# A graph network kernel on one core: the message sum as products of split operands, moved behind two state products

## The chip, the cores and the metric

The kernel runs on one core of a Trainium2 chip. The metric is the device time of one execution in microseconds, the median over runs. TensorE (PE) multiplies into PSUM, VectorE (DVE), ScalarE (ACT) and GpSimd (POOL) do the elementwise work, SyncE (SP) issues the loads and stores. Each engine works through its own instruction list in order; the lists meet at semaphores.

## The reference, cut to what matters

Sixteen graphs of 512 nodes with 128 features, each with a 512x512 weighted adjacency.

```python
x = x + L0_gnn(layernorm(x), adj)          # relu(norm_adj @ (x W + b))
x = x + layernorm(x) @ Wf.T + bf
x = x + L1_gnn(layernorm(x), adj)          # below
x = x + L1_ffn(layernorm(x))               # 30 steps of tanh, silu, layernorm, 128x128 product

# L1_gnn, per graph:
x_conv = relu(conv17(relu(conv1(x))) + x)          # with folded batch norms
A   = exp(-dist(s, s)) * mask                       # s = x w_se.T; mask is adj: the edges
msg = relu(x @ w_msg.T + b_msg)
x_nmp = A @ msg                                     # the edge-weighted message sum
gi, gh = [x_conv, x_nmp] @ w_ih.T + b_ih, x @ w_hh.T + b_hh
r, z = sigmoid(gi_r + gh_r), sigmoid(gi_z + gh_z)
out = (1 - z) * tanh(gi_n + r * gh_n) + z * x
```

## The kernel before, in words

Two stages: the graph stage (to about 545 us), one step per graph, and the 30 feed-forward iterations, which work on all nodes in eight groups. The change touches the graph stage only.

A step `step(b, p, c, d)` does, software pipelined, the L1 graph layer of graph b, the L0 graph layer and linear layer of graph c = b + 1, and the adjacency of graph d = b + 2. There is no planner: the order of every engine is written out by hand in its own `step` function (POOL L544, PE L713, ACT L1035, DVE L1426). A wait therefore holds everything behind it on its engine. Steps 0 and 1 and the last ones are written apart; the middle ones run in a loop.

Numbers: a plain fp32 product is one call with fp32 operands. Where the kernel wants the other way it keeps an operand as two parts of type fp32r, the high part (a copy rounded to fp32r, by ScalarE) and the low part (the operand less the high part, by VectorE or POOL), and `product` (L676) issues three matmuls: high x high, high x low, low x high. conv1, the convolution, the state products (HH, three gates on x) and the input products (IH, on x_conv and x_nmp) are of that kind. The message sum (L844 to 851) is not: four fp32 products of 128x512, one for each edge tile mt, out of `msg_tok` and `edge`.

Order on TensorE in the last third of a step: distances 0 and 1, adjacency turns 0 and 1 (transposes into the banks TURN_A and TURN_B), turn(1) of the layernorm, distances 2 and 3, the linear layer's products, the last convolution tap, the message sum, turns 2 and 3, nine matmuls of the state products (DIST_A, DIST_B, TURN_B), six of x_conv, turn(2), then the x_nmp products and the next step's conv1.

What feeds them. ScalarE: exp(0..3) into `edge`, adjacency copies 0 and 2 out of TURN_A (`adjt_even`), the two relus of x_conv, x_nmp's high part, gates. VectorE: edge products 1 and 3 (L1306, edge times adjacency), adjacency copies 1 and 3 out of TURN_B (`adjt_odd`, L1302), statistics (L1264) and norms (L1295), conv_sum (L1422), x_nmp's low part (L1568). POOL: edge products 0 and 2 (L509), the small `rstd` pairs (L503, L505) between statistics and norms, x_conv's low part (L596). The third turn waits for the first copy, as both use TURN_A. Each adjacency copy overwrites the tile from which the step's edge products are made: `adj_t[p]` is shared by graphs b and d, and a copy of any tile waits for all of the step's edge products (L990 to 994, L1299 to 1302).

Of the kernel before, what the change touches and what calls it, by code (L numbers as in the profile page):

```python
# [27 lines left out]
P = 128  # L28
# [63 lines left out]
def build(nc, x, adj, w0, b0, wf, bf, w_se, b_se, conv1_w, bn1, conv2_w, bn2, w_msg, b_msg,  # L92
          w_ih, b_ih, w_hh, b_hh, ln_w, ln_b, w1, b1, out):
    with ExitStack() as ctx:
# [26 lines left out]

            return sba(name + "_h", shape, F32R), sba(name + "_l", shape, F32R)

        work = sba("work", [P, 20 * N])

        def piece(first, count):
            return work[:, first * N:(first + count) * N]
# [52 lines left out]

        emb_m = sba("emb_m", [KD, N], F32R)
        emb_n = sba("emb_n", [KD, N], F32R)
        emb_f = [[sba(f"emb_f{w}{k}", [KD, N]) for k in range(2)] for w in range(2)]
        msg_tok = sba("msg_tok", [P, NT, C])
        conv_pre = sba("conv_pre", [P, N])
        x_conv = split("x_conv", [P, N])
        x_nmp = split("x_nmp", [P, N])
        n_act = sba("n_act", [P, N])
        upd = sba("upd", [P, N])


# [83 lines left out]
        s_exp = sem("s_exp")  # L275
        s_edge_p = sem("s_edge_p")
        s_edge_v = sem("s_edge_v")
        s_nmp = sem("s_nmp")
        s_x_nmp = sem("s_x_nmp")
        s_x_nmp_lo = sem("s_x_nmp_lo")  # L280
# [189 lines left out]
        def _(pool):  # L470
# [36 lines left out]
            def edges(b, p, mt):  # L507
                pool.wait_ge(s_exp, 4 * b + mt + 1)
                pool.tensor_tensor(edge[:, mt, :], edge[:, mt, :], adj_t[p][:, mt, :], ALU.mult).then_inc(s_edge_p, 1)  # L509

            def power(j):
                pool.wait_ge(f_v, j + 1)
                half = slice(GT * (j % 2), GT * (j % 2) + GT)
                pool.tensor_tensor(f_rs[:, both(j), half], f_var[:, j, :], half_neg[:, 0:GT], ALU.pow).then_inc(f_pow, 1)
# [29 lines left out]
            def step(b, p, c, d):  # L544
                l1 = exists(b)
                if l1:

                    pool.wait_ge(s_h1, 2 * b + 1)
                    if c is not None:
                        pool.wait_ge(s_xs, c + 1)  # L550
                    inner = slice(EDGE, EDGE + INNER)
                    odd = phases(h_full[:])[:, 1, inner]
                    for k in range(2):
                        even = phases(h_full[:, 2 * k:2 * k + 2 * (EDGE + INNER)])[:, 0, inner]
                        ins = pool.tensor_tensor(diff[:, k, inner], even, odd, ALU.subtract)
                    ins.then_inc(s_diff, 1)
                    pool.wait_ge(s_diff_hi, b + 1)
                    pool.tensor_tensor(diff_s[1][:, :, inner], diff[:, :, inner], diff_s[0][:, :, inner].bitcast(F32),
                                       ALU.subtract).then_inc(s_diff_lo, 1)
                    for w in range(2):  # L560
                        pool.wait_ge(s_emb_sg, 2 * b + w + 1)
                        pool.tensor_tensor(emb_f[w][0][:], emb_f[w][0][:], emb_f[w][1][:], ALU.mult).then_inc(s_emb_v, 1)

                if b is None and c is not None:
                    pool.wait_ge(s_wload, 16 * NWEIGHTS)

                    pool.wait_ge(s_xs, 1)
                    for k in range(SUM_FILLS):
                        even, odd = (conv2_nat[:, :, 8 * k + h:8 * k + h + 7:2].rearrange("p i t -> p t i") for h in range(2))
                        pool.tensor_tensor(sum_nat[k], even, odd, ALU.add).then_inc(s_sums, 1)  # L570
                if c is not None:
                    rstd(1, c)
                if b is None:
                    rstd(0, d)
                if b is None and c is not None:
                    vectors()
                if l1:
                    if c is not None:

                        pool.wait_ge(s_norm[1], c + 1)  # L580
                    edges(b, p, 0)
                if later(b) and not ends(b, B - 1):
                    rstd(3, b - 1)
                if ends(b, B):
                    power(2)
                    power(3)
                    centre(2, 2)
                if l1:
                    edges(b, p, 2)
                if c is not None:  # L590
                    rstd(2, c)
# [27 lines left out]
        def _(pe):  # L619
# [93 lines left out]
            def step(b, p, c, d):  # L713
# [126 lines left out]
                        pe.wait_ge(s_rows_read, 1)  # L840
                    turn_adjacency(0, 2)
                if l1:

                    pe.wait_ge(s_msg_tok, b + 1)  # L844
                    for mt in range(NT):
                        if mt % 2 == 0:
                            pe.wait_ge(s_edge_p, 2 * b + mt // 2 + 1)
                        else:
                            pe.wait_ge(s_edge_v, 2 * b + mt // 2 + 1)
                        m = pe.matmul(bank[CHAN], msg_tok[:, mt, :], edge[:, mt, :], start=(mt == 0), stop=(mt == NT - 1))  # L850
                    m.then_inc(s_nmp, 1)
                if d is not None:
                    turn_adjacency(2, NT)
                if l1:
                    x_in = cut(xc_s, 0, N)

                    pe.wait_ge(s_exp, 4 * b + 4)
                    product(bank[DIST_A], w(HH), x_in, stop=False)
                    product(bank[DIST_B], w(HH + 1), x_in, stop=False)
                    if d is not None:  # L860
                        pe.wait_ge(s_adjt_odd, 2 * d + 2)
                    elif not l0:
                        pe.wait_ge(s_gh_n, b)
# [95 lines left out]
        def _(act):  # L959
# [29 lines left out]

            def adjt_even(c, q, mt):  # L990
                act.wait_ge(s_adj_turned, 4 * c + mt + 1)
                wait(act, s_edge_p, 2 * (c - 1))
                wait(act, s_edge_v, 2 * (c - 1))
                act.activation(adj_t[q][:, mt, :], bank[TURN_A], ACT.Copy).then_inc(s_adjt_even, 1)

            def exp(b, mt):
                act.wait_ge(s_dist, 4 * b + mt + 1)
                wait(act, s_nmp, b)
                act.activation(edge[:, mt, :], bank[DIST_A + mt % 2], ACT.Exp).then_inc(s_exp, 1)  # L999

            def silu(j, s):
                act.wait_ge(f_u, s + 1)
# [32 lines left out]
            def step(b, p, c, d):  # L1035
# [37 lines left out]
                if l1:  # L1073
# [4 lines left out]
                        act.activation(emb[:], emb_f[m][0][:], ACT.Copy).then_inc(s_emb_hi, 1)  # L1078
                    act.wait_ge(s_msg_pre, b + 1)
                    wait(act, s_nmp, b)  # L1080
                    act.activation(msg_tok[:], msg_tok[:], ACT.Relu).then_inc(s_msg_tok, 1)
                    if ends(b, B - 1):
                        silu(0, 0)
                        silu(1, 1)
# [11 lines left out]
                if l1:  # L1096
                    exp(b, 2)
                    exp(b, 3)
                if d is not None:
                    adjt_even(d, p, 0)  # L1100
                if l1:
                    act.wait_ge(s_conv_pre, b + 1)
                    wait(act, s_z_ps, b)
                    act.activation(x_conv[0][:], conv_pre[:], ACT.Relu, bias=vec(SH2)).then_inc(s_x_conv, 1)
# [1 line left out]
                    act.activation(conv_pre[:], conv_pre[:], ACT.Relu, bias=vec(SH2)).then_inc(s_x_conv, 1)  # L1106
                if ends(b, B - 1):
                    tanh(0, 2)
                if l1:
                    act.wait_ge(s_nmp, b + 1)  # L1110
                    act.activation(x_nmp[0][:], bank[CHAN], ACT.Copy).then_inc(s_x_nmp, 1)
                if ends(b, B - 1):
                    tanh(0, 3)
                if d is not None:
                    adjt_even(d, p, 2)
                if l1:

                    act.wait_ge(s_ghn_ps, b + 1)
# [30 lines left out]
        def _(dve):  # L1149
# [148 lines left out]

            def adjt_odd(c, q, mt):  # L1299
                dve.wait_ge(s_adj_turned, 4 * c + mt + 1)  # L1300
                wait(dve, s_edge_p, 2 * (c - 1))
                dve.tensor_copy(adj_t[q][:, mt, :], bank[TURN_B]).then_inc(s_adjt_odd, 1)  # L1302

            def edges(b, p, mt):
                dve.wait_ge(s_exp, 4 * b + mt + 1)
                dve.tensor_tensor(edge[:, mt, :], edge[:, mt, :], adj_t[p][:, mt, :], ALU.mult).then_inc(s_edge_v, 1)  # L1306

            def statistics_of(j, s, q):
                if q == 0:
# [116 lines left out]
            def step(b, p, c, d):  # L1426
# [96 lines left out]
                    conv_sum(b)  # L1523
                if l1:
                    edges(b, p, 1)
                if later(b) and not ends(b, B - 1):
                    dve.wait_ge(s_x3, b)
                    stats(3, b - 1)
# [2 lines left out]
                if l0:  # L1531
# [1 line left out]
                    dve.tensor_tensor(x_graph(c), x_graph(c), tiles(bank[TOK]), ALU.add).then_inc(s_x2, 1)  # L1533
                    dve.wait_ge(s_x2, c + 1)
                    stats(2, c)
                if d is not None:
                    adjt_odd(d, p, 1)
                if l1 and not ends(b, B - 1):
                    conv_sum(b)
                if ends(b, B - 1):  # L1540
                    statistics(1, 1)
                    scaled_sum(0, 2)
# [77 lines left out]
```

## Time and profile before

| | us |
|---|---|
| median of 3 runs | 1264.63 (1263.76 to 1265.21) |
| the profiled execution's own time | 1265.02 |
| its span, first to last instruction | 1263.0 |
| busy: PE, DVE, ACT, POOL | 1228.0, 1151.7, 960.0, 947.3 |
| mean granted TensorE clock | 0.993 of full |

How to read the rows: a timeline row has start and duration in us, the engine, the line of the kernel, the operation, the tile written and the tiles read, and how many such instructions are merged (x4 means the duration runs over four). Square brackets tell how long the engine was idle before it and which instruction, on which line, ended the wait. A matmul's duration contains its drain, so the cost of one in a stream is the distance between starts. The tile `work` holds the adjacency, its copies and `edge` in one buffer; names alone do not tell them apart, lines do.

### The profile page before, as it was taken

To read this page: it belongs to the slowest core of one execution; us is meant where nothing else is said; L and a number is where in the kernel's file an instruction comes from. 1 tells how busy PE (TensorE), PEld (TensorE's weight loads), DVE (VectorE), ACT (ScalarE), POOL (GpSimd) and SP (SyncE) were. 2 spreads that over 40 slices of the span, in tenths; PEclk is the share of its full clock that TensorE was granted. 3 is DMA by queue.
4 is the path that set the end of the run, shared out by engine and by line. 5 is a ranking of instruction groups with operands and counts; after the bars stand their busy time and mean duration, and the time that the engine had idled before them with its cause. 6 is when DMAs were issued, how large, how long until landed. Compare 5 with 4: busy or idle time off the path is not lost.

```text
span 1263.0 us, 27914 instructions
## 1 busy us (share of the span) xinstructions
PE 1228.0 (97%) x9073; PEld 1094.9 (87%) x9073; DVE 1151.7 (91%) x3029; ACT 960.0 (76%) x1170; POOL 947.3 (75%) x667
## 2 busy tenths in 40 slices
PE   8899999999999999869999999999999999999998
PEld 7677777777777777659999999999999999999998
DVE  7988888888888887789999999999999999999996
ACT  2455555555555555769999999999999999999994
POOL 2455555555555555579999999999999999999996
PEclk9999999999999999979999999999999999999999
DMA  6111111111111000000000000000000000000004
GB/s 196 43 43 42 43 42 42 42 42 42 43 42 46 35 0 1 1 1 1 1 0 0 0 0 0 0 0 0 0 0 0 0 0 0 0 0 0 0 0 133
DMA packets 29812, 27.77 MB, mean 22 GB/s; under 512 B 3285, under 2 KB 21464, under 8 KB 29656
## 3 DMA queue, kind: packets, MB, share of 16 engines
q1 hardware_dynamic: 29784, 27.41, 6.9%
q8 instruction: 16, 0.26, 0.1%
q14 instruction: 12, 0.10, 0.0%
HBM read 23.21 MB, written 4.19 MB: 22 GB/s over the span
## 4 chain that ended last, share of the span: by engine, by line
PE 74%; DVE 13%; issue 5%; ACT 4%; POOL 3%; DVEq 0%; DMA 0%; SPq 0%; POOLq 0%; ACTq 0%
PE psum L894 28%; PE psum L946 15%; PE psum L679 4%; PE psum L681 4%; PE psum L680 4%; PE psum L850 4%; PE psum L911 3%; PE psum L701 3%; PE psum L696 3%; POOL h_ring L533 2%; DVE emb_n L1507 2%; DVE xh_mem L1295 1%; PE psum L690 1%; ACT emb_f L1054 1%; DVE u_ring L1329 1%
## 5 line engine op out<-in xcount | busy, mean ns | idle before, releaser
L533 POOL TENSOR_TENSOR h_ring<-g_pair,f_rs 128x1024 f32<-128x1024 f32 x240 | 451.9, 1904 | 31.5 <-DVE f_rs L1400 19.0
L1312 DVE BATCH_NORM_STATS2 f_stat<-g_pair 128x6 f32<-128x256 f32 x960 | 394.5, 425 | 2.4 <-ACT g_pair L1003 2.4
L946 PE MATMUL psum<-ident,h_ring 128*128 128x128 f32 (+1 forms) x1920 | 296.8, 277 | 7.8 <-POOL h_ring L533 6.8
L1329 DVE SCALAR_TENSOR_TENSOR u_ring<-t_ring,psum 128x1024 f32<-128x1024 f32 x232 | 281.9, 1215 | 8.1 <-ACT t_ring L1013 3.6
L946 PEld LDWEIGHTS psum<-ident,h_ring 128*128 128x128 f32 (+1 forms) x1920 | 247.7, 167 | 35.1 <-issue 7.1
L1017 ACT ACTIVATE y_all<-psum 128x1024 f32<-128x1024 f32 x240 | 244.0, 1017 | 17.2 <-PE psum L946 17.2
L894 PE MATMUL psum<-w_t,y_all 128*128 128x128 f32 x1920 | 254.5, 276 | 0.0
L894 PE MATMUL psum<-w1c_t,y_all 128*128 128x128 f32 x1920 | 253.8, 275 | 0.0
L1003 ACT ACTIVATE g_pair<-u_ring 128x1024 f32<-128x1024 f32 x240 | 251.7, 1049 | 0.9 <-DVE u_ring L1329 0.9
L1013 ACT ACTIVATE t_ring<-psum 128x1024 f32<-128x1024 f32 x232 | 238.1, 1026 | 15.6 <-PE psum L894 8.9
L894 PEld LDWEIGHTS psum<-w_t,y_all 128*128 128x128 f32 x1920 | 234.3, 192 | 0.0
L894 PEld LDWEIGHTS psum<-w1c_t,y_all 128*128 128x128 f32 x1920 | 233.7, 192 | 0.0
L523 POOL TENSOR_TENSOR g_pair<-g_pair,f_stat 128x1024 f32<-128x1024 f32 x120 | 229.8, 1915 | 0.0
L503 POOL TENSOR_SCALAR ln_ve<-ln_stat 128x4 f32<-128x4 f32 x64 | 19.4, 303 | 135.9 <-DVE ln_stat L1264 135.9
L999 ACT ACTIVATE work<-psum 128x512 f32<-128x512 f32 x64 | 34.8, 595 | 96.1 <-PE psum L761 96.0
L911 PE MATMUL psum<-bias,ones_bf 65*128 65x512 bf16 x240 | 91.9, 383 | 0.0
L679 PE MATMUL psum<-diff_s_h,wt_h 128*128 128x256 f32 x272 | 81.2, 299 | 0.0
L680 PE MATMUL psum<-diff_s_l,wt_h 128*128 128x256 f32 x272 | 76.4, 281 | 0.0
L681 PE MATMUL psum<-diff_s_h,wt_l 128*128 128x256 f32 x272 | 76.3, 280 | 0.0
L505 POOL TENSOR_TENSOR ln_rs<-ln_ve,half_neg 128x4 f32<-128x4 f32 x64 | 71.7, 1120 | 5.3
L509 POOL TENSOR_TENSOR work<-work 128x512 f32<-128x512 f32 x32 | 46.5, 1456 | 32.7 <-DVE xh_mem L1295 25.4
L1366 DVE TENSOR_REDUCE f_share<-psum 128x16 f32<-128x48 f32 x354 | 67.5, 191 | 0.1
(200 smaller groups left out, 2146.7 us busy)
## 6 DMA issues: line engine op xcount, KB each, us to landing
work<-in_adj_dram SPq DMA_DIRECT2D x16, 1024.0 KB, 5.5
x_tok<-in_x_dram SPq DMA_DIRECT2D x16, 256.0 KB, 5.6
out_dram<-y_all SPq DMA_DIRECT2D x7, 512.0 KB, 3.2
work<-in_L_gnn_conv_w_dram SPq DMA_DIRECT2D x1, 1088.0 KB
out_dram<-y_all SPq DMA_DIRECT2D x2, 256.0 KB, 3.6
work<-in_L_gnn_w_ih_dram SPq DMA_DIRECT2D x1, 384.0 KB
work<-in_L_gnn_w_hh_dram SPq DMA_DIRECT2D x1, 192.0 KB
work<-in_L_gnn_W_dram SPq DMA_DIRECT2D x1, 64.0 KB, 5.1
```

The source lines that it names most:

```text
L523: pool.tensor_tensor(two, two, means, ALU.subtract).then_inc(f_mean, 1)
L533: pool.tensor_tensor(tiles(h_ring[j % 4]), tiles(g_ring[j]), spread(f_rs[:, both(j), at:at + GT], GT, C), ALU.mult).then_inc(f_norm, 1)
L679: pe.matmul(dst, lhs[0], rhs[0], start=start, stop=False)
L680: pe.matmul(dst, lhs[0], rhs[1], start=False, stop=False)
L894: m = pe.matmul(y_ps[k % 2][:, h, C * t:C * t + C], y_all[:, GT * k + NT * h + t, :], w1c_t[:] if h == centred(k) else w1_t[:], start=(h = ...
L911: pe.matmul(y_ps[k % 2][:, 1 - centred(k), :].rearrange("p (o n) -> p o n", o=2), ones_bf[:], four, start=True, stop=False, skip_group_che ...
L946: m = pe.transpose(g_ps[j % 2][0:rows, t // NT, P * (t % NT):P * (t % NT) + P], tiles(h_ring[j % 4])[:, t, 0:rows], ident[:])
L1003: act.activation(g_ring[j], u_ring[j % 2], ACT.Silu).then_inc(f_silu, 1)
L1013: act.activation(t_ring[k % 2], src, ACT.Tanh).then_inc(f_tanh, 1)
L1017: act.activation(y_all[:, GT * j:GT * j + GT, :].rearrange("p t c -> p (t c)"), g_ps[j % 2].rearrange("p h n -> p (h n)"), ACT.Copy).then_ ...
L1312: ins = dve.bn_stats(f_stat[:, j, 0, 2 * q:2 * q + 2, :].rearrange("p t w -> p (t w)"), two)
L1329: dve.scalar_tensor_tensor(out=u_ring[k % 2], in0=t_ring[k % 2], scalar=STEP, in1=src, op0=ALU.mult, op1=ALU.add).then_inc(f_u, 1)
```

## The change

The messages and the edges are split into high and low parts, and each edge tile's sum is a `product` of three matmuls, in the order 1, 0, 3, 2. The state products of r and z and turns 2 and 3 go ahead of the message sum. ScalarE makes the high parts, with a new wait for the update of graph b-1 (whose `n_act` shares memory with `msg_h`); the low parts of edges 0 and 2 and of the messages go to POOL, those of edges 1 and 3 to VectorE. An adjacency copy waits only for the edge product of its own tile; copy 1 on VectorE and copy 2 on ScalarE come earlier in their lists. Buffers: `edge_l` lies over `edge`, `edge_h` over `emb_f`, `msg_l` over `msg_tok`, `msg_h` over `n_act`.

```diff
 # POOL
+            def edge_low(b, mt):
+                pool.wait_ge(s_edge_hi_p, 2 * b + mt // 2 + 1)
+                pool.tensor_tensor(edge_l[:, mt, :], edge[:, mt, :], edge_h[:, mt, :].bitcast(F32),
+                                   ALU.subtract).then_inc(s_edge_lo_p, 1)
+            def msg_low(b):
+                pool.wait_ge(s_msg_hi, 2 * b + 2)
+                pool.tensor_tensor(msg_l[:], msg_tok[:], msg_h[:].bitcast(F32),
+                                   ALU.subtract).then_inc(s_msg_tok, 1)
...
+                if l1:
+                    msg_low(b)
                 if c is not None:
                     rstd(1, c)
...
                 if l1:
                     edges(b, p, 2)
+                    edge_low(b, 0)
+                    edge_low(b, 2)
                 if c is not None:
                     rstd(2, c)
 # PE
                 if l1:
-                    pe.wait_ge(s_msg_tok, b + 1)
-                    for mt in range(NT):
-                        if mt % 2 == 0:
-                            pe.wait_ge(s_edge_p, 2 * b + mt // 2 + 1)
-                        else:
-                            pe.wait_ge(s_edge_v, 2 * b + mt // 2 + 1)
-                        m = pe.matmul(bank[CHAN], msg_tok[:, mt, :], edge[:, mt, :], start=(mt == 0), stop=(mt == NT - 1))
-                    m.then_inc(s_nmp, 1)
-                if d is not None:
-                    turn_adjacency(2, NT)
-                if l1:
                     x_in = cut(xc_s, 0, N)
                     pe.wait_ge(s_exp, 4 * b + 4)
                     product(bank[DIST_A], w(HH), x_in, stop=False)
                     product(bank[DIST_B], w(HH + 1), x_in, stop=False)
+                if d is not None:
+                    turn_adjacency(2, NT)
+                if l1:
+                    pe.wait_ge(s_msg_tok, b + 1)
+                    for mt in (1, 0, 3, 2):
+                        if mt % 2 == 0:
+                            pe.wait_ge(s_edge_lo_p, 2 * b + mt // 2 + 1)
+                        else:
+                            pe.wait_ge(s_edge_lo_v, 2 * b + mt // 2 + 1)
+                        m = product(bank[CHAN], (msg_h[:, mt, :], msg_l[:, mt, :]), (edge_h[:, mt, :], edge_l[:, mt, :]),
+                                    start=(mt == 1), stop=(mt == 2))
+                    m.then_inc(s_nmp, 1)
 # ACT
             def adjt_even(c, q, mt):
                 act.wait_ge(s_adj_turned, 4 * c + mt + 1)
-                wait(act, s_edge_p, 2 * (c - 1))
-                wait(act, s_edge_v, 2 * (c - 1))
+                if isinstance(c, int) and c < 2:
+                    pass
+                else:
+                    act.wait_ge(s_edge_p, 2 * (c - 2) + mt // 2 + 1)
...
+                    if later(b):
+                        act.wait_ge(s_upd, b)
+                    act.activation(msg_h[:], msg_tok[:], ACT.Relu).then_inc(s_msg_hi, 1)
+                    act.wait_ge(s_msg_hi, 2 * b + 1)
+                    act.activation(msg_tok[:], msg_tok[:], ACT.Relu).then_inc(s_msg_hi, 1)
...
                     exp(b, 3)
+                    edge_high(b, 0)
                 if d is not None:
                     adjt_even(d, p, 0)
                 if l1:
+                    edge_high(b, 1)
+                    edge_high(b, 3)
+                    edge_high(b, 2)
                     act.wait_ge(s_conv_pre, b + 1)
 # DVE
             def adjt_odd(c, q, mt):
-                wait(dve, s_edge_p, 2 * (c - 1))
+                if not (isinstance(c, int) and c < 2):
+                    dve.wait_ge(s_edge_v, 2 * (c - 2) + mt // 2 + 1)
...
                 if l1:
                     edges(b, p, 1)
+                if d is not None and l1:
+                    adjt_odd(d, p, 1)
...
-                if d is not None:
+                if d is not None and not l1:
                     adjt_odd(d, p, 1)
+                if l1:
+                    edge_low(b, 1)
                 if l1 and not ends(b, B - 1):
                     conv_sum(b)
+                if l1:
+                    edge_low(b, 3)
```

`edge_high` on ScalarE is a Copy of one edge tile to fp32r behind that tile's edge product; VectorE's `edge_low` is POOL's with its own semaphores. On ScalarE `adjt_even(d, p, 2)` moves from behind x_nmp's high part to before it.

## Rows read from the trace of the kernel before

**Rows 1.** Busy time by stretch: stretch, length, PE, PEld, DVE, ACT, POOL, clock.
```profile
60.00:480.00 420.00, 416.91 (x2442) 330.27 (x2441) 351.80 (x672) 217.06 (x363) 216.08 (x244) 1.00 0.12 38
```

**Rows 2.** Timeline of TensorE, step 8 and the start of step 9.
```profile
289.85 0.40 PE L679 MATMUL psum<-xc_s_h,wt_h 128*128 128x512 f32 x1
...
309.93 3.60 PE L850 MATMUL psum<-work,msg_tok 128*128 128x512 f32 x8
313.36 1.04 PE L710 MATMUL psum<-ident,work 128*128 128x128 f32 x8
...
316.33 0.40 PE L679 MATMUL psum<-x_conv_h,wt_h 128*128 128x512 f32 x1
...
317.74 0.60 PE L690 MATMUL psum<-ident,xh_mem 128*128 128x128 f32 x4
318.24 0.47 PE L679 MATMUL psum<-x_nmp_h,wt_h 128*128 128x512 f32 x1
...
321.13 0.39 PE L679 MATMUL psum<-xc_s_h,wt_h 128*128 128x512 f32 x1
```

**Rows 3.** Timeline of POOL, step 8.
```profile
304.11 1.43 POOL L505 TENSOR_TENSOR ln_rs<-ln_ve,half_neg 128x4 f32<-128x4 f32 x1
307.28 1.64 POOL L509 TENSOR_TENSOR work<-work 128x512 f32<-128x512 f32 x1 [1.74 <-DVE xh_mem L1295]
...
310.14 1.30 POOL L509 TENSOR_TENSOR work<-work 128x512 f32<-128x512 f32 x1
...
312.31 1.07 POOL L505 TENSOR_TENSOR ln_rs<-ln_ve,half_neg 128x4 f32<-128x4 f32 x1
314.68 1.29 POOL L596 TENSOR_TENSOR x_conv_l<-conv_pre,x_conv_h 128x512 fp32r<-128x512 f32 x1 [1.30 <-ACT conv_pre L1106]
```

**Rows 4.** Timeline of VectorE, step 8, and two rows of step 9.
```profile
307.08 0.69 DVE L1306 TENSOR_TENSOR work<-work 128x512 f32<-128x512 f32 x1
...
309.63 0.69 DVE L1306 TENSOR_TENSOR work<-work 128x512 f32<-128x512 f32 x1 [1.17 <-ACT work L999]
...
311.07 0.76 DVE L1264 BATCH_NORM_STATS2 ln_stat<-x_tok 128x6 f32 x2 [0.15 <-DVE x_tok L1533]
311.75 0.68 DVE L1302 COPY work<-psum 128x512 f32<-128x512 f32 x1
312.34 0.75 DVE L1422 SCALAR_TENSOR_TENSOR conv_pre<-psum,bcol,conv_pre 128x512 f32<-128x512 f32 x1
...
315.04 1.78 DVE L1295 TENSOR_SCALAR xh_mem<-x_tok,ln_stat,ln_rs 128x128 f32 x4
...
317.42 0.67 DVE L1568 TENSOR_TENSOR x_nmp_l<-psum,x_nmp_h 128x512 fp32r<-128x512 f32 x1
...
330.79 0.69 DVE L1479 SCALAR_TENSOR_TENSOR upd<-upd,n_act 128x512 f32<-128x512 f32 x1
...
332.77 0.69 DVE L1496 SCALAR_TENSOR_TENSOR x_tok<-agg_tok,x_tok 128x512 f32 x1
```

**Rows 5.** Timeline of ScalarE, step 8.
```profile
297.81 0.64 ACT L1078 ACTIVATE emb_m<-emb_f 105x512 fp32r<-105x512 f32 x1
...
305.96 1.09 ACT L999 ACTIVATE work<-psum 128x512 f32<-128x512 f32 x2 [6.47 <-PE psum L761]
...
311.48 0.60 ACT L994 ACTIVATE work<-psum 128x512 f32<-128x512 f32 x1 [1.88 <-POOL work L509]
```

**Rows 6.** Timeline of VectorE, step 0 and step 15.
```profile
59.59 1.38 DVE L1306 TENSOR_TENSOR work<-work 128x512 f32<-128x512 f32 x1 [0.62 <-ACT work L999]
...
514.65 0.69 DVE L1476 SCALAR_TENSOR_TENSOR upd<-gates,upd 128x512 f32<-128x512 f32 x1
515.38 1.66 DVE L1479 SCALAR_TENSOR_TENSOR upd<-upd,n_act 128x512 f32<-128x512 f32 x1
```

**Rows 7.** Timeline of POOL, step 0 and step 15.
```profile
59.15 1.27 POOL L509 TENSOR_TENSOR work<-work 128x512 f32<-128x512 f32 x1 [0.73 <-ACT work L999]
...
514.72 1.76 POOL L562 TENSOR_TENSOR emb_f<-emb_f 105x512 f32<-105x512 f32 x1 [0.65 <-ACT emb_f L1054]
```

More of the change, by code:

```diff
@@ L122, in split @@
             return sba(name + "_h", shape, F32R), sba(name + "_l", shape, F32R)
-        work = sba("work", [P, 20 * N])
+        with ExitStack() as under:
+            work = under.enter_context(nc.sbuf_tensor("work", [P, 20 * N], F32))
+        sba("work_below", [P, 16 * N])
+        edge_l = sba("edge_l", [P, NT, N], F32R)
         def piece(first, count):
@@ L182, in build @@
         emb_n = sba("emb_n", [KD, N], F32R)
-        emb_f = [[sba(f"emb_f{w}{k}", [KD, N]) for k in range(2)] for w in range(2)]
-        msg_tok = sba("msg_tok", [P, NT, C])
+        with ExitStack() as under:
+            emb_f = [[under.enter_context(nc.sbuf_tensor(f"emb_f{w}{k}", [KD, N], F32)) for k in range(2)] for w in range(2)]
+            msg_tok = under.enter_context(nc.sbuf_tensor("msg_tok", [P, NT, C], F32))
+        edge_h = sba("edge_h", [P, NT, N], F32R)
+        msg_l = sba("msg_l", [P, NT, C], F32R)
         conv_pre = sba("conv_pre", [P, N])
@@ L187, in build @@
         x_nmp = split("x_nmp", [P, N])
-        n_act = sba("n_act", [P, N])
+        with ExitStack() as under:
+            n_act = under.enter_context(nc.sbuf_tensor("n_act", [P, N], F32))
+        msg_h = sba("msg_h", [P, NT, C], F32R)
         upd = sba("upd", [P, N])
@@ L277, in build @@
         s_edge_v = sem("s_edge_v")
+        s_edge_hi_p = sem("s_edge_hi_p")
+        s_edge_hi_v = sem("s_edge_hi_v")
+        s_edge_lo_p = sem("s_edge_lo_p")
+        s_edge_lo_v = sem("s_edge_lo_v")
+        s_msg_hi = sem("s_msg_hi")
         s_nmp = sem("s_nmp")
@@ L999, in exp, with edge_high @@
                 act.activation(edge[:, mt, :], bank[DIST_A + mt % 2], ACT.Exp).then_inc(s_exp, 1)
+            def edge_high(b, mt):
+                if mt % 2 == 0:
+                    act.wait_ge(s_edge_p, 2 * b + mt // 2 + 1)
+                else:
+                    act.wait_ge(s_edge_v, 2 * b + mt // 2 + 1)
+                act.activation(edge_h[:, mt, :], edge[:, mt, :], ACT.Copy).then_inc(s_edge_hi_p if mt % 2 == 0 else s_edge_hi_v, 1)
             def silu(j, s):
@@ L1080, in step @@
                     wait(act, s_nmp, b)
-                    act.activation(msg_tok[:], msg_tok[:], ACT.Relu).then_inc(s_msg_tok, 1)
+                    if later(b):
[3 more added lines that the diff above has]
+                    act.activation(msg_tok[:], msg_tok[:], ACT.Relu).then_inc(s_msg_hi, 1)
                     if ends(b, B - 1):
@@ L1108, in step @@
                     tanh(0, 2)
+                if d is not None:
+                    adjt_even(d, p, 2)
                 if l1:
@@ L1113, in step @@
                     tanh(0, 3)
-                if d is not None:
-                    adjt_even(d, p, 2)
                 if l1:
@@ L1306, in edges, with edge_low @@
                 dve.tensor_tensor(edge[:, mt, :], edge[:, mt, :], adj_t[p][:, mt, :], ALU.mult).then_inc(s_edge_v, 1)
+            def edge_low(b, mt):
+                dve.wait_ge(s_edge_hi_v, 2 * b + mt // 2 + 1)
+                dve.tensor_tensor(edge_l[:, mt, :], edge[:, mt, :], edge_h[:, mt, :].bitcast(F32),
+                                  ALU.subtract).then_inc(s_edge_lo_v, 1)
             def statistics_of(j, s, q):
@@ L1535, in step @@
                     stats(2, c)
-                if d is not None:
+                if d is not None and not l1:
                     adjt_odd(d, p, 1)
+                if l1:
+                    edge_low(b, 1)
                 if l1 and not ends(b, B - 1):
                     conv_sum(b)
+                if l1:
+                    edge_low(b, 3)
                 if ends(b, B - 1):
```

## The prediction

> **What bounds the kernel now.** I read the busy time by stretches first. From 60 to 480 us, the graph stage in its steady state, TensorE is busy 416.91 of 420.00 us at full granted clock; VectorE is at 352, ScalarE at 217, POOL (GpSimd) at 216 [rows 1]. So there TensorE's order of work is the time, and another engine costs only what it makes TensorE wait. I followed one of the sixteen steps, b = 8, in the timeline of each engine. TensorE starts its conv1 product at 289.85 and the next step's at 321.13: a period of 31.28 us [rows 2]. In it: message products 309.93 to 313.36 (3.43 us for four fp32 products, eight records), two adjacency turns and nine state products to 316.33, six x_conv products to 317.74 (1.41, so 0.235 each), a turn, and the x_nmp products from 318.24. All times below are of this step.
>
> Two cross-engine inputs arrive only just in time there. x_conv_l ends on POOL at 314.68 + 1.29 = 315.97 [rows 3], 0.36 before TensorE takes it. x_nmp_l ends on VectorE at 317.42 + 0.67 = 318.09 [rows 4], 0.15 before TensorE takes it. These two margins are what the change must not eat.
>
> **TensorE's part.** Four fp32 products (3.43 us) go; twelve fp32r products of 128x512 come, 12 x 0.235 = 2.82. The state products and turns only change places. Gain 0.61 us a step, 16 x 0.61 = 9.8 us in all, if nothing waits. By that order the state products of r and z run 309.93 to 311.34, the turns (2.97 for turns and nine products, less 9 x 0.235: 0.85) to 312.2, messages to 315.0, the third state product to 315.7, and TensorE would want x_conv_l at 315.7 and x_nmp_l at 317.6.
>
> **What comes on the other engines, per step.**
> - ScalarE: four edge roundings and one more message rounding, at the 0.64 of a copy of that kind [rows 5]: 3.2 us. It is half idle, and the message pair runs in the 6.47 us in which it waits for the distances: its new wait for upd (331.48 in step 9, so 300.2 here [rows 4]) holds only the first exp behind it, at 305.96. The edge roundings stand behind the last exp (309.6) with the first adjacency copy between them, five operations at about 0.6: three are done by 311.8, the last waits for POOL's second edge product. Nothing queued behind them is late: x_conv waits for conv_sum anyway. Cost 0 by itself.
> - The adjacency copies wait only for their own tile. ScalarE's 1.88 us wait before the first copy [rows 5] goes; it was idle time of an engine with room, so 0. But the copy is now behind one rounding (done about 310.8), which TensorE needs before the third turn at 311.34: covered by 0.5. The adjacency loads on SP's queue, released by the turns, go out some 2 us earlier, as the turns now come before the messages; their first reader is in the next step. 0.
> - VectorE: two edge_low of 0.69 (the kind of its edge product, two SBUF inputs); a copy of 0.68 moves forward, ahead of the statistics for graph b-1 [rows 4].
> - POOL: msg_low and two edge_low, each a 128x512 difference, at the 1.30 of x_conv_l and of the second edge product [rows 3]: 3.9 us. The two edge_low stand in POOL's queue behind its second edge product and ahead of rstd(2) and of x_conv_l. That is the step of the change which I hold to decide.
>
> **POOL's queue alone, a floor.** From the first edge product's start at 307.28 nothing before is changed. Then 1.64 (blocked as now), rstd(3) 1.3 (its second operation is 1.07, the first and the gap 0.2), edge product 1.30, two edge_low 2.60, rstd(2) 1.3, x_conv_l 1.29: 9.4 us without any wait, so x_conv_l is not done before 316.7, where TensorE had begun on it at 316.33. The rest up to the next step is fixed TensorE work: +0.4 us a step at least, though TensorE has 0.61 less to do. With rstd(3) half a us later, since its statistics stand behind the moved copy, it is 317.25 and +1.0.
>
> **The two engines block one another.** At 59.15 POOL's edge product runs to 60.42; VectorE's, started at 59.59, takes 1.38 instead of 0.69 and ends at 60.97, 0.55 after POOL's. In step 8 POOL's first edge product takes 1.64 and ends 1.15 after VectorE's (307.77). At 514.65 VectorE, then POOL, then VectorE alternate: POOL's operation of 514.72 ends 1.14 after VectorE's, and VectorE's next, issued at 515.38, 0.56 after POOL's [rows 3, 4, 6, 7]. So a VectorE operation with two SBUF inputs and a POOL operation exclude each other, and the one that waits goes next. The Trainium skill says it as well (SBUF — State Buffer, section "SBUF: two separate sides"): the shared port pair is an exclusive lock held for the whole instruction, against VectorE operations with two SBUF inputs among others. It speaks against putting edge_low on both engines at once. The rows agree with the lock, but a blocked VectorE product ends 0.55 after POOL, not its full 0.69; with full durations after each release the four hand-overs below would add 0.6 us, +2.8 a step, 1307, inside the forecast's own range.
>
> With these lags (VectorE 0.55 after POOL's end, POOL 1.15 after VectorE's), the tail of the step, written out:
> 1. rstd(3): statistics at 309.15, POOL's two small operations to 310.6, or 311.05 if the second takes 1.43 as at 304.11, where VectorE was busy beside it [rows 3]. Second edge product to 312.1 (middle).
> 2. VectorE's edge_low(1) is ready at 311.83, blocked, ends 312.65; TensorE waits for it from 312.2.
> 3. POOL edge_low(0) to 313.8. VectorE's conv_sum (0.75, PSUM, unblocked) meanwhile; edge_low(3) blocked to 314.35.
> 4. POOL edge_low(2) to 315.5; TensorE ends the messages at about 316.35. VectorE's norm(3) is blocked to 316.45, and the adjacency copy behind it ends at 317.05: TensorE's third state product waits for that.
> 5. rstd(2) about 316.8, x_conv_l 318.1; the x_conv products and the turn run to 320.0.
> 6. norm(2) contends with x_conv_l as now (from 315.04 it takes 1.78 and ends 0.85 after x_conv_l): 318.95. Statistics 0.68 (as from 311.07 to the copy), x_nmp_l 0.67: 320.3. TensorE's x_nmp products at 320.45 where they were at 318.24: +2.2 us a step.
>
> Behind that point TensorE's work is as before, and what other engines do for it starts from it. The short and the long end of rstd(3) and rstd(2) (1.07 or 1.43) make +1.9 to +2.6.
>
> **msg_low** can start about 1.44 after upd's end: two roundings of 0.64 and hand-overs of 0.16. VectorE's x_tok sum, which has two SBUF inputs, starts 1.29 after it (step 9: upd ends at 331.48, the sum starts at 332.77) [rows 4]. VectorE is first, by little; msg_low then ends 1.15 after the sum, about when VectorE wants its next such operation: I take 0. Were POOL first, the sum would be blocked until 0.55 after msg_low, 1.45 + 1.30 + 0.55 = 3.3 after upd's end instead of 1.98: 1.3 late, and with it the chain to the embeddings and to norm(1), which TensorE takes just in time.
>
> **Sum.** Steps 1 to 13 are alike: 13 x 2.2 = 28.6. Steps 0, 14 and 15 lack part of the queue (rstd(3), the adjacency, rstd(2)): 1.5 each, between the 0.4 and the 2.2: 4.5. The second phase from 560 us is untouched. 33 us over the profiled execution's 1265.02 (span 1263.0): 1298, which stands 0.4 us higher than from the median 1264.63.
>
> **Rivals.**
> - Only POOL's queue counts, because the contenders mostly miss each other: +0.4 to +1.0 a step, 16 x 1.0 = 16, so 1271 to 1281. For it: the operations are pinned to different releasers, and a shift of 0.3 us avoids a block. Against: both engines have their edge_low ready within 0.3 us of each other. Chance 0.22.
> - POOL wins msg_low against the x_tok sum: 1.3 more in up to 13 steps, 1305 to 1315. For it: 0.15 us is all that parts them. Against: VectorE is the earlier. Chance 0.10.
> - The other side: POOL's differences hide in its idle time, and the 0.61 on TensorE shows: 1265 - 9.8 = 1255. The place is x_conv_l; it decides from the point where POOL ends it by 315.7. POOL is idle 1.30 before x_conv_l, and about 0.6 between its edge product's end (311.44) and rstd(2), 1.9 in all against 2.6 added, and it would have to be done 0.27 earlier than now; each edge_low would have to take about 0.8. No row shows a POOL operation of that size under 1.27. Chance 0.08. That gain and loss cancel: 0.04.
>
> Forecast 0.56. It alone: 1288 to 1308. The range for 8 in 10 takes in most of the first rival and part of the second: 1272 to 1311. About 0.2% (2.5 us) can be told from no change. Faster 0.08, same 0.04, slower 0.88.
>
> **What would show it.** Right: a period near 33.5; TensorE waits before x_conv and x_nmp products named by x_conv_l on POOL and x_nmp_l or the adjacency copy on VectorE; edge_low on VectorE at 0.9 to 1.3 instead of 0.69, norm(3) longer by a POOL operation; message products 0.235 apart where they do not wait. Wrong: x_conv_l ending before 316 in step 8's scale, VectorE's edge_low at 0.69 throughout, or a period under 31.28. The granted clock should stay at 1.00 with waits under 1 us.

## The result, and the profile after

The changed kernel takes 1304.04 us (median of 4 runs, 1303.09 to 1305.92); the kernel before, on the same chip, 1264.46. The ratio is 1.0314 [1.0301, 1.0327]: slower by 39.6 us, where the prediction said 33. The profiled execution took 1303.09 with a span of 1301.3. Times are medians of executions; of the run at 1262.86 below, one execution of ten took 1521.49 at a granted clock of 0.75, and its ratio leaves that one out.

The page, busy time by engine, and its chain of waits (before: PE 74%, DVE 13%, POOL 3%):

```profile
PE 1236.6 (95%) x9137; PEld 1103.7 (85%) x9137; DVE 1205.2 (93%) x3061; ACT 1006.6 (77%) x1250; POOL 1033.2 (79%) x715
...
PE 62%; DVE 15%; POOL 11%; issue 7%; ACT 4%; DVEq 1%; DMA 0%; SPq 0%; POOLq 0%; ACTq 0%
```

Busy time by stretch, the stretch and columns of [rows 1]. TensorE's busy time fell by 21 us and is no longer the whole stretch; the clock is the same, so this is waiting:

```profile
60.00:480.00 420.00, 395.70 (x2314) 313.29 (x2313) 371.78 (x651) 238.53 (x401) 270.84 (x265) 1.00 0.12 38
```

What TensorE waited for from 60 to 500 us (line <- engine, tile, line: us in total, times, longest). Before, this view has 3.9 us for the norm and 0.3 for x_conv_l, and nothing else:

```profile
PE psum L706 <- DVE edge_l L1356: 10.9, 14, 1.9
PE psum L706 <- DVE work L1348: 5.9, 12, 0.5
PE psum L717 <- DVE xh_mem L1340: 3.0, 13, 0.2
PE psum L706 <- POOL x_conv_l L623: 2.1, 12, 0.2
PE psum L706 <- POOL edge_l L526: 2.1, 12, 0.2
```

Step 8 of TensorE, answering to [rows 2]; conv1 starts at 307.38 and at 341.06, a period of 33.68 where it was 31.28:

```profile
307.38 0.40 PE L706 MATMUL psum<-xc_s_h,wt_h 128*128 128x512 f32 x1
...
330.59 0.50 PE L706 MATMUL psum<-edge_h,msg_h 128*128 128x512 f32 x1 [0.69 <-DVE edge_l L1356]
330.93 0.40 PE L707 MATMUL psum<-edge_l,msg_h 128*128 128x512 f32 x1
331.16 0.39 PE L708 MATMUL psum<-edge_h,msg_l 128*128 128x512 f32 x1
331.74 0.50 PE L706 MATMUL psum<-edge_h,msg_h 128*128 128x512 f32 x1 [0.18 <-POOL edge_l L526]
332.08 0.40 PE L707 MATMUL psum<-edge_l,msg_h 128*128 128x512 f32 x1
...
334.01 0.40 PE L708 MATMUL psum<-edge_h,msg_l 128*128 128x512 f32 x1
334.90 0.50 PE L706 MATMUL psum<-xc_s_h,wt_h 128*128 128x512 f32 x1 [0.49 <-DVE work L1348]
335.24 0.39 PE L707 MATMUL psum<-xc_s_l,wt_h 128*128 128x512 f32 x1
...
336.04 0.47 PE L706 MATMUL psum<-x_conv_h,wt_h 128*128 128x512 f32 x1 [0.18 <-POOL x_conv_l L623]
...
338.17 0.48 PE L706 MATMUL psum<-x_nmp_h,wt_h 128*128 128x512 f32 x1
...
341.06 0.39 PE L706 MATMUL psum<-xc_s_h,wt_h 128*128 128x512 f32 x1
```

The same step of POOL, answering to [rows 3], and behind it the second operation of rstd(3) in that step before the change:

```profile
319.21 1.76 POOL L531 TENSOR_TENSOR msg_l<-msg_tok,msg_h 128x512 fp32r<-128x512 f32 x1 [3.49 <-ACT msg_tok L1122]
...
327.20 1.55 POOL L518 TENSOR_TENSOR ln_rs<-ln_ve,half_neg 128x4 f32<-128x4 f32 x1
328.72 1.27 POOL L522 TENSOR_TENSOR work<-work 128x512 f32<-128x512 f32 x1
329.95 3.44 POOL L526 TENSOR_TENSOR edge_l<-work,edge_h 128x512 fp32r<-128x512 f32 x2
...
334.61 1.28 POOL L623 TENSOR_TENSOR x_conv_l<-conv_pre,x_conv_h 128x512 fp32r<-128x512 f32 x1
```

```profile
309.16 1.01 POOL L505 TENSOR_TENSOR ln_rs<-ln_ve,half_neg 128x4 f32<-128x4 f32 x1
```

And of VectorE, answering to [rows 4]:

```profile
324.63 0.69 DVE L1352 TENSOR_TENSOR work<-work 128x512 f32<-128x512 f32 x1
...
327.19 0.69 DVE L1352 TENSOR_TENSOR work<-work 128x512 f32<-128x512 f32 x1 [0.46 <-ACT work L1029]
...
329.31 1.23 DVE L1356 TENSOR_TENSOR edge_l<-work,edge_h 128x512 fp32r<-128x512 f32 x1
330.46 0.74 DVE L1473 SCALAR_TENSOR_TENSOR conv_pre<-psum,bcol,conv_pre 128x512 f32<-128x512 f32 x1
331.12 1.11 DVE L1356 TENSOR_TENSOR edge_l<-work,edge_h 128x512 fp32r<-128x512 f32 x1
332.16 2.09 DVE L1340 TENSOR_SCALAR y_all<-x_tok,ln_stat,ln_rs  x4
334.17 0.68 DVE L1348 COPY work<-psum 128x512 f32<-128x512 f32 x1
334.77 1.98 DVE L1340 TENSOR_SCALAR xh_mem<-x_tok,ln_stat,ln_rs 128x128 f32 x4
```

VectorE and POOL alternate: from 329.3 to 336.8 VectorE's two edge_low take 1.23 and 1.11 and its two norms (four operations each) 2.09 and 1.98, while conv_sum and the adjacency copy, which read PSUM, keep 0.74 and 0.68.

### The profile page after: what moved, and what is told of

It is laid out like the page before. It is cut to its first block, busy times and chain, and to the rows that moved or that the text cites. A ratio compares the mean times of both kernels' runs of the same rounds, so it can differ in the third digit from the quotient of the medians.

```text
span 1301.3 us, 28190 instructions
## 1 busy us (share of the span) xinstructions
PE 1236.6 (95%) x9137; PEld 1103.7 (85%) x9137; DVE 1205.2 (93%) x3061; ACT 1006.6 (77%) x1250; POOL 1033.2 (79%) x715
## 4 chain that ended last, share of the span: by engine, by line
PE 62%; DVE 15%; POOL 11%; issue 7%; ACT 4%; DVEq 1%; DMA 0%; SPq 0%; POOLq 0%; ACTq 0%
PE psum L922 28%; PE psum L974 14%; PE psum L706 4%; PE psum L939 3%; PE psum L708 3%; PE psum L707 3%; PE psum L728 3%; POOL edge_l L526 3%; POOL h_ring L556 2%; POOL ln_rs L518 2%; DVE emb_n L1558 2%; PE psum L723 2%; POOL work L522 1%; POOL x_conv_l L623 1%; DVE xh_mem L1340 1%
## 5 line engine op out<-in xcount | busy, mean ns | idle before, releaser
L518 POOL TENSOR_TENSOR ln_rs<-ln_ve,half_neg 128x4 f32<-128x4 f32 x64 | 77.8, 1215 | 5.3
L531 POOL TENSOR_TENSOR msg_l<-msg_tok,msg_h 128x512 fp32r<-128x512 f32 x16 | 26.7, 1671 | 52.8 <-ACT msg_tok L1122 52.8
```

## The experiments

Ratios are to the kernel before, run on the same chip beside each. "Waits" are TensorE's from 60 to 500 us.

**Where the low parts of the edges are made.** All four on VectorE:

```diff
 # POOL
-                    edge_low(b, 0)
-                    edge_low(b, 2)
...
 # DVE
...
                     edge_low(b, 1)
+                    edge_low(b, 0)
...
                     conv_sum(b)
...
                     edge_low(b, 3)
+                    edge_low(b, 2)
```

> The changed kernel with all four edge_low on VectorE; POOL makes none. Theory (the edge_low operations exclude one another across VectorE and POOL, and stand in POOL's list before x_conv_l): no alternation, edge_low at 0.69 each, x_conv_l near its old place; what is left is VectorE's list, four operations longer, so TensorE takes x_nmp about 1.2 us later than in the kernel before: period 32.5, about 1285 us. Rival A (only the length of POOL's list counts, VectorE has room): back to 1265 or below. Rival B (the new order on TensorE and the moved adjacency copies cost the time): 1304 stays.

1302.09, ratio 1.0289 [1.0272, 1.0306]: a miss, and close to the 1304 of rival B, which the run of the order alone, below, sets aside. Its waits, and VectorE and POOL late in a step:

```profile
PE psum L704 <- DVE work L1346: 18.6, 12, 1.6
PE psum L704 <- DVE edge_l L1354: 11.6, 24, 0.9
```

```profile
334.21 2.08 DVE L1338 TENSOR_SCALAR y_all<-x_tok,ln_stat,ln_rs  x4
336.21 0.68 DVE L1346 COPY work<-psum 128x512 f32<-128x512 f32 x1
```

```profile
334.68 1.27 POOL L621 TENSOR_TENSOR x_conv_l<-conv_pre,x_conv_h 128x512 fp32r<-128x512 f32 x1 [1.39 <-ACT conv_pre L1149]
```

POOL has room and TensorE no longer waits for x_conv_l at all, yet only 2 us are won: norm(3) now meets x_conv_l, and the adjacency copy, which TensorE needs, stands behind it. POOL's queue is not by itself what costs. The other way, all four on POOL:

```diff
 # POOL
-                    edge_low(b, 0)
-                    edge_low(b, 2)
+                    for mt in (1, 0, 3, 2):
+                        edge_low(b, mt)
...
 # DVE
...
-                    edge_low(b, 1)
...
-                    edge_low(b, 3)
```

> The changed kernel with all four edge_low on POOL. Theory: POOL's list before x_conv_l is 2.6 us longer than in the changed kernel, less what the alternation cost it (about 0.9): x_conv_l decides, period 35 to 35.5, 1325 to 1332 us. Rival A (POOL's list alone, nothing gained by the end of the alternation): 2.6 more a step, 1345. Rival B (order on TensorE): 1304.

1328.17, ratio 1.0498 [1.048, 1.0515], as expected: 26.0 us of wait for edge_low on POOL and 9.9 for x_conv_l.

**No low part of the edges; and the order alone.**

Both engines' edge_low go, and TensorE waits for the high parts alone:

```diff
...
-                        m = product(bank[CHAN], (msg_h[:, mt, :], msg_l[:, mt, :]), (edge_h[:, mt, :], edge_l[:, mt, :]),
-                                    start=(mt == 1), stop=(mt == 2))
+                        pe.matmul(bank[CHAN], msg_h[:, mt, :], edge_h[:, mt, :], start=(mt == 1), stop=False)
+                        m = pe.matmul(bank[CHAN], msg_l[:, mt, :], edge_h[:, mt, :], start=False, stop=(mt == 2))
...
```

> The changed kernel without the low part of the edges: no edge_low on either engine and two matmuls for a tile instead of three (left out: the low part of the edge weights). Theory: x_conv_l and x_nmp_l are back at their old places, and since these two bound the step even before, TensorE's 1.55 us fewer per step hardly show: 1258 to 1268. Rival (TensorE's work decides as soon as the low parts are gone): 1265 less 16 x 1.55, 1240. Rival B (order on TensorE, copies): 1300.

1262.86, ratio 0.9982 [0.9972, 0.9992], inside the range given. So the four edge_low with their four products carry 41.2 us, all of the loss; roundings, message split, copies and order together cost nothing, net of what the cheaper products save. TensorE now has 1.55 us a step less to do than before (3.43 less 8 x 0.235), but gains 0.1: it waits 14.3 us for x_conv_l, whose place is set by the lists.

The kernel before with the changed order of TensorE and the per-tile copies, and the four fp32 products:

```diff
...
+                    product(bank[DIST_A], w(HH), x_in, stop=False)
+                    product(bank[DIST_B], w(HH + 1), x_in, stop=False)
...
+                    turn_adjacency(2, NT)
...
-                    for mt in range(NT):
+                    for mt in (1, 0, 3, 2):
...
-                        m = pe.matmul(bank[CHAN], msg_tok[:, mt, :], edge[:, mt, :], start=(mt == 0), stop=(mt == NT - 1))
+                        m = pe.matmul(bank[CHAN], msg_tok[:, mt, :], edge[:, mt, :], start=(mt == 1), stop=(mt == 2))
...
```

> The kernel before with only the order of the change: state products of r and z and the adjacency turns ahead of the fp32 message sum, adjacency copies that wait for their own tile and stand earlier; no split. Theory: nothing but places move on TensorE, x_nmp's chain is still met: 1262 to 1269. Rival B (the order, with less work behind the message sum to cover x_nmp's way, costs the time): 1285 to 1304.

1263.24, ratio 0.9988 [0.9978, 0.9997], inside the range given: these parts of the change save about 1.5 us, if anything.

**What the exclusion costs.** VectorE's edge_low takes its first input from PSUM:

```diff
...
+                    src = bank[CONV] if mt == 1 else bank[TURN_B]
-                dve.tensor_tensor(edge_l[:, mt, :], edge[:, mt, :], edge_h[:, mt, :].bitcast(F32),
+                dve.tensor_tensor(edge_l[:, mt, :], src, edge_h[:, mt, :].bitcast(F32),
...
```

> The changed kernel, same operations in the same lists, but in steps 0 to 13 VectorE's two edge_low take their first input from PSUM instead of SBUF (left out by that: the true low part of edge tiles 1 and 3). Theory (exclusion between POOL and VectorE operations with two SBUF inputs): VectorE's edge_low drop from 1.11 to about 0.68 and POOL's from 1.74 to about 1.30, x_conv_l ends about 1 us earlier, period 32.7, about 1290 us. Rival A (the length of the lists alone): both durations and the 1304 stay.

1291.54, ratio 1.0205 [1.0188, 1.0222], as expected. The two engines' edge_low by form (min/median/max in ns), in the changed kernel and in this one:

```profile
L526 POOL TENSOR_TENSOR edge_l<-work,edge_h x32: 1261/1736/1753, 60.0 to 563.7; 128x512 fp32r<-128x512 f32 x32
L1356 DVE TENSOR_TENSOR edge_l<-work,edge_h x32: 677/1114/1634, 62.0 to 563.2; 128x512 fp32r<-128x512 f32 x32
```

```profile
L526 POOL TENSOR_TENSOR edge_l<-work,edge_h x32: 1269/1288/1752, 60.2 to 552.4; 128x512 fp32r<-128x512 f32 x32
L1361 DVE TENSOR_TENSOR edge_l<-psum,edge_h x28: 668/676/694, 62.2 to 487.0; 128x512 fp32r<-128x512 f32 x28
```

With one input from PSUM the two engines' edge_low are free of each other, 0.44 us shorter on either. That is shown; it is worth 12.5 of the 39.6 us. The rest stays with free-running edge_low: the work itself, in two lists with no room there, and the norms, which are still blocked (its norm(3) takes 2.19). No run separates these two.

**Moving one thing.** norm(3) behind x_nmp_l, so that the adjacency copy doesn't stand behind it:

```diff
-                if later(b) and not ends(b, B - 1):
+                if later(b) and not ends(b, B - 1) and not l1:
                     norm(3, b - 1)
...
                     dve.tensor_tensor(x_nmp[1][:], bank[CHAN], x_nmp[0][:].bitcast(F32), ALU.subtract).then_inc(s_x_nmp_lo, 1)
+                if l1 and later(b) and not ends(b, B - 1):
+                    norm(3, b - 1)
```

> The changed kernel with VectorE's norm(3), which nothing in the step needs, behind x_nmp_l instead of ahead of the last adjacency copy. Theory (x_conv_l on POOL and norm(2) behind it end the step): TensorE's wait of 0.49 for the copy goes, and comes back before x_conv and x_nmp: 1300 to 1304. Rival (norm(3), blocked by POOL, is itself what delays the step, as it seems to do with all edge_low on VectorE): 14 x 0.6 less, 1295.

1305.94, ratio 1.0322 [1.0305, 1.034], 1.9 above the range given and far from the rival's 1295. The wait for the copy (5.9) is gone and that for x_conv_l grew from 2.1 to 11.0: the wait moved. The mirror image, x_conv_l ahead of rstd(2) on POOL:

```diff
                     edge_low(b, 2)
-                if c is not None:
-                    rstd(2, c)
                 if l1:
                     pool.wait_ge(s_x_conv, 2 * b + 2)
                     ...
+                if c is not None:
+                    rstd(2, c)
```

> The changed kernel with one move: x_conv_l ahead of rstd(2) on POOL. By the prediction's tail rstd(2) (1.3) stands before x_conv_l, which ends 2.3 late; but TensorE's third state product waits for the adjacency copy (about 2.4 late by the blocked norm(3)) ahead of it, and the norm(2) behind rstd(2) comes later. So the wait for x_conv_l goes and those for edge_low and the copy stay, norm(2) and x_nmp_l move 0.3 to 1.3 later: 1296 to 1312, little changed or worse. Rival, POOL's queue alone: 13 times up to 1.3 less, 1287 to 1292.

1315.3, ratio 1.0397 [1.038, 1.0414], slower still and above the range given. Its waits, and its norm(3):

```profile
PE psum L706 <- DVE work L1348: 17.7, 12, 1.5
PE psum L706 <- DVE edge_l L1356: 10.3, 13, 1.9
```

```profile
337.41 3.06 DVE L1340 TENSOR_SCALAR y_all<-x_tok,ln_stat,ln_rs  x4
```

Now x_conv_l follows the edge_low pair without a gap, norm(3) stands beside both and takes 3.06 instead of 2.09, and the copy is 1 us later. In the changed kernel the small rstd operations stand between the two, and VectorE's norms run on beside them.

**Other lists, all low parts on VectorE.** First, the statistics of graph c behind three low parts, those of d and norm(3) last:

```diff
...
+                    edge_low(b, 1)
...
+                    conv_sum(b)
...
+                    edge_low(b, 0)
+                    edge_low(b, 3)
...
                     stats(2, c)
...
+                    edge_low(b, 2)
...
```

> All edge_low on VectorE as in e1_low_dve, and VectorE's list by what TensorE needs first: edge_low(1), conv_sum, edge_low(0), edge_low(3), statistics of graph c, edge_low(2), the copy, norm(2), x_nmp_l, and only then the statistics of d and norm(3). Theory (in e1_low_dve it was norm(3), blocked by x_conv_l, ahead of the copy; VectorE's work that TensorE needs fits): x_nmp at 0 to 0.5 us behind the kernel before, 1265 to 1275. Rival (VectorE has too much work between the last exp and x_nmp_l in any order): 1290 to 1302.

1293.14, ratio 1.0218 [1.0201, 1.0235]: a miss. Waits, and what POOL does before x_conv_l:

```profile
PE psum L704 <- POOL x_conv_l L621: 11.4, 14, 0.8
PE psum L704 <- DVE edge_l L1354: 10.5, 28, 0.6
```

```profile
328.32 0.45 POOL L516 TENSOR_SCALAR ln_ve<-ln_stat 128x4 f32<-128x4 f32 x1 [2.04 <-DVE ln_stat L1307]
```

POOL sits idle for 2.04 until the later statistics come, and x_conv_l stands behind them. So x_conv_l went ahead of rstd(2), conv_sum ahead of the x_tok sum, x_nmp_l ahead of norm(2):

> All four low parts of the edges on VectorE, as in the run that reordered VectorE's list, and now also x_conv_l ahead of rstd(2) on POOL, conv_sum ahead of the x_tok sum and x_nmp_l ahead of norm(2) on VectorE. My theory, that the time of the changed kernel is the order of the lists around x_conv_l and the adjacency copy: TensorE's 11.4 us of wait for x_conv_l go (0.8 a step), of its 10.5 for edge_low most stays, and the time falls from 1293 to 1270 to 1283, still not under the kernel before, because four low parts more stand on VectorE before x_nmp_l (each 0.69). Rival, that the low parts themselves are too much work for the tail whatever the order: the wait moves to edge_low or to x_nmp_l at the same size, 1288 to 1298. Second rival, that the order was all of it: 1255, TensorE's 0.61 us a step gained.

1297.66, ratio 1.026 [1.0243, 1.0277], a miss, and worse. The earlier x_conv_l (329.34 to 330.62 on POOL) meets the last edge_low, which takes 1.58 for 0.69, and TensorE waits for it:

```profile
329.59 1.58 DVE L1354 TENSOR_TENSOR edge_l<-work,edge_h 128x512 fp32r<-128x512 f32 x1
```

```profile
331.23 0.50 PE L704 MATMUL psum<-edge_h,msg_h 128*128 128x512 f32 x1 [1.03 <-DVE edge_l L1354]
```

Then the four low parts as early as their inputs allow (1, 0, the x_tok sum, 3, 2), the copy next, the statistics of c behind it:

> The run with all low parts on VectorE and the reordered lists took 1297.66, because its last low part of an edge met x_conv_l on POOL (1.58 us instead of 0.69; TensorE waited 1.03 for it) and its first came 0.70 late behind the x_tok sum. Here the four low parts stand as early as their inputs allow (1, 0, the x_tok sum, 3, 2), then the adjacency copy, and the statistics of graph c behind it; x_conv_l stays ahead of rstd(2). My theory, that each of these waits is one meeting in the lists: both go, 1.4 us a step, 13 times: 1275 to 1285, with a small new wait for norm(2) at turn(2). Rival, that VectorE's tail is too long whatever the order: the wait comes back at turn(2) or x_nmp_l, 1290 to 1300.

1291.84, ratio 1.0209 [1.0192, 1.0226], a miss again, and what the rival said. Waits, and the first pair of low parts:

```profile
PE psum L715 <- DVE xh_mem L1338: 13.7, 27, 0.9
PE psum L704 <- DVE edge_l L1354: 11.0, 27, 0.7
```

```profile
323.14 2.39 DVE L1354 TENSOR_TENSOR edge_l<-work,edge_h 128x512 fp32r<-128x512 f32 x2 [0.17 <-ACT edge_h L1034]
```

The meeting of the last low part with x_conv_l is gone. The first pair meets POOL's edge product instead (2.39 for two), and the statistics, being later, make norm(2) late for its turn. Four orders gave 1292 to 1302, and each of the last three came out inside the range of its rival, that VectorE's tail is too long in any order: with these low parts there, each place frees one wait and opens another. That no order can do it is not shown; four were tried.

**A version without the work.** The edge product itself writes fp32r, so the edges have no low part and ScalarE rounds nothing; the messages stay split, two products a tile. Lists nearly as in the run of 1297.66 (the statistics of c directly behind the x_tok sum), without edge_low:

```diff
-                dve.tensor_tensor(edge[:, mt, :], edge[:, mt, :], adj_t[p][:, mt, :], ALU.mult).then_inc(s_edge_v, 1)
+                dve.tensor_tensor(edge_l[:, mt, :], edge[:, mt, :], adj_t[p][:, mt, :], ALU.mult).then_inc(s_edge_v, 1)
...
+                        pe.matmul(bank[CHAN], msg_h[:, mt, :], edge_l[:, mt, :], start=(mt == 1), stop=False)
+                        m = pe.matmul(bank[CHAN], msg_l[:, mt, :], edge_l[:, mt, :], start=False, stop=(mt == 2))
```

> Edges rounded once: the edge products on POOL and VectorE write fp32r, no edge_high and no edge_low, two matmuls for a tile (left out: the low part of the edge weights); conv_sum ahead of the x_tok sum, x_conv_l ahead of rstd(2), x_nmp_l ahead of norm(2), statistics of d and norm(3) last. Theory (in e3_no_low TensorE waited only for x_conv_l, which stands behind conv_sum, edge_high and rstd(2)): x_nmp about 1.2 us earlier than before, 1240 to 1250. Rival (something else of the step is as late): 1258 to 1263.

1250.77, ratio 0.9888 [0.9872, 0.9905], 0.8 above the range given: faster than both kernels. Of its waits of more than a single time one row is left:

```profile
PE psum L715 <- DVE xh_mem L1334: 9.9, 29, 1.1
```

Its control, the same lists with the four fp32 products:

> The kernel before with the changed order on TensorE and the changed adjacency copies, and with the lists of the kernel whose edge product writes the rounded edges directly (x_conv_l ahead of rstd(2), conv_sum ahead of the x_tok sum, x_nmp_l ahead of norm(2), statistics of d and norm(3) last), but with the four fp32 message products. It is the control for that kernel's gain. If the gain (about 14 us) is the cheaper message product, as I hold, this one is bound by TensorE as the kernel before: 1260 to 1265. If the lists alone made it, about 1250.

1271.96, ratio 1.0058 [1.0042, 1.0075]: slower by 7 us, above the 1260 to 1265 expected (it waits 8.7 us for the norms, of which the lists made one later). So the gain is not the lists'. Side by side:

| message sum | lists of the change | other lists |
|---|---|---|
| four fp32 products | 1263.24 | 1271.96 |
| two products a tile, no low part of the edges | 1262.86 | 1250.77 |

Neither gains alone: cheaper products only turn into a wait for x_conv_l, and the other lists only delay the norms. The last entry also lacks ScalarE's four roundings; what they are worth there no run shows.

## Why the prediction was right, and where not

The direction and the range were right, and the loss came out 6.6 us above the 33 forecast. The tail that it wrote out, set against the trace (VectorE's edge product starts at 324.63, at 307.08 in [rows 4], so 17.55 is taken off):

| step 8, us | predicted | measured |
|---|---|---|
| POOL's second edge product ends | 312.1 | 312.44 |
| edge_low(1) ends | 312.65 | 312.99 |
| edge_low(3) ends | 314.35 | 314.68 |
| POOL's edge_low(2) ends | 315.5 | 315.84 |
| norm(3) ends | 316.45 | 316.70 |
| adjacency copy ends | 317.05 | 317.30 |
| x_conv_l ends | 318.1 | 318.34 |
| norm(2) ends | 318.95 | 319.20 |
| x_nmp products start | 320.45 | 320.62 |

- **The exclusion and its lags** held: from row to row the distances are those written, to within 0.1. The 1307 of full durations after each release lies nearer to 1304.04, but not for that reason: edge_low(1) ends 0.55 after POOL's product, as written, and not 0.69. The whole column is 0.17 to 0.34 late from its first row on. That is rstd(3): its second operation took 1.55 (327.20), outside the 1.07 to 1.43 given, and 1.01 before. VectorE's second edge product had begun 0.01 ahead of it (327.19); before, that product began 0.47 behind it (309.63 in [rows 4]). The run of the order alone, in which the copy and the statistics behind it stand in the same places, has 1.55 in this step as well. That the product is what holds it up is read from these traces; no run tests it alone. The period grew by 2.40, not 2.2, inside +1.9 to +2.6.
- **msg_low costs nothing**: held. It was POOL that was blocked (1.76); VectorE's x_tok sum went first, by 0.07 us in step 8 (319.14 and 319.21), so the rival that gave POOL the first turn was missed by little; and the wait before turn(1) is still 0.23.
- **TensorE's 0.61** a step is there (0.235 between starts where nothing waits) and is lost in the waits, as is the 1.55 of the run without low parts.
- **The clock** stays 1.00 from 60 to 480 us, as forecast.
- **"That step of the change which I hold to decide"**, POOL's two edge_low ahead of rstd(2) and x_conv_l, was right in its time and too narrow as a cause. TensorE waits least for x_conv_l (2.1 us) and most for edge_low and the copy; with POOL relieved, and VectorE loaded instead, the time was 1302. The two engines' lists end about equally late and hold each other up, so moving low parts from one to the other wins 2 us or costs 24. The rival "POOL's queue alone" falls with it: the run with free-running edge_low is still at 1291.54, above its 1281.
- **The sum.** By the traces, of 38.3 us in span: steps 1 to 13 gave 31.4 (28.6 predicted); steps 0, 14 and 15 gave 1.0, 1.9 and 2.2, so 5.1 (4.5 predicted); -0.4 before step 0. The rest, 2.2, is the hand-over to the feed-forward stage, which the prediction held to be untouched; this is the term that it lacks. TensorE's last wait for the update grew from 6.8 to 8.3: of that, 0.86 is the norm into y_all ahead of the update, which takes 1.97 beside POOL's work of the next stage, 1.11 before. Behind that wait four transposes take 1.06 instead of 0.60, at a granted clock of 0.53 from 576 to 586 us, that is mostly at the lower level of 1.2 GHz, after 8.26 us without work; before, it was 0.67 from 540 to 560, after 6.75.

## What to carry to other kernels

Splitting an operand moves work from the full engine to those that feed it. Before doing so, write out the tail of each feeding engine up to the operand that TensorE takes last, with the operations that exclude each other laid end to end. If two lists there have no room, moving work between them or within them mostly changes the name of the wait (here it won back 12 of 40 us at best); take the work away (here, let the operation that makes the operand write it rounded, which gives up that operand's low part), and then reorder.

## What was not expected of the hardware

- A stop of TensorE cost more than the wait named for it. From 331.16 over 331.74 to 332.08 are 0.92 us where two starts in a stream are 0.47 apart: 0.45 lost for a wait of 0.18. At 334.90, 0.76 for 0.49. So 0.27 comes on top of each of these two stops, at full clock, and 0.24 at that for x_conv_l (336.04). Some 0.16 of it is how the wait is counted: it begins at the end of the last matmul (0.39 to 0.40 long), while in a stream the next one would have started 0.235 after that one's start. The other 0.1 is the start after the stop, 0.34 to the next matmul instead of 0.235. Counted by starts, the stops make about 2.9 of the 3.0 us that step 8 loses (2.40 and the hidden 0.61); the waits view names 1.54 of them.
- Norms, VectorE operations with one tensor input in SBUF, are blocked as well; the prediction's rule names two SBUF inputs, though its tail has the norms blocked. Four take 1.11 alone, 1.78 to 2.19 beside one 128x512 operation of POOL, ending 0.85 to 0.86 after it, and 3.06 beside an edge_low and x_conv_l that follow without a gap. One beside a small rstd operation alone keeps its 1.11 (from 313.00 before, beside rstd(2)). Statistics (0.76 to 0.78) and operations with an input in PSUM (0.67 to 0.75) are not blocked.
